# A block of attention and experts on one core: weight splitting, the last batch's scatters, shared inputs and results rearranged

## The chip, the core and the metric

The kernel runs on one core of a Trainium2 chip, as one launch. The metric is the device time of one execution, in microseconds. The engines are TensorE (PE), VectorE (DVE), ScalarE (ACT), GpSimd (POOL) and SyncE (SP); each runs its own list of instructions in order, and semaphores tie the lists together.

## The reference

The input x has 16 batches of 512 tokens with 128 features. The block is two sublayers, each with a residual and a layer norm behind it:

```python
q = plucker(q1, q2); k = plucker(k1, k2)        # 16 heads, 6 line coordinates each, unit length
attn = softmax(causal(q @ (J k)^T * 6**-0.5))
x1 = layernorm(x + (attn @ v) @ Wo.T + bo)
cw = top-2 of sigmoid(x1 @ Wr.T + rb), of 8 experts
out = expert_shared(x1) + sum_e cw[e] * expert_e(x1)   # expert: silu(x Wg^T) * (x Wu^T) @ Wd^T
y = layernorm(x1 + out)
```

There are nine experts with three matrices of 128 x 256 each: the shared one (number 0 in the weight buffer) and eight routed ones. Only the two chosen of the eight are computed for a token.

## The kernel before

**Attention stage.** One body per batch b, on every engine, from `over_batches` (L217): batches 0 to 3 are written out, 4 to 13 are a loop of two, 14 and 15 are written out. Heads go in four groups g, the scores of a group in five chunks of 128 x 1024 in PSUM. TensorE makes a chunk (`scores`, L662), ScalarE takes its exponential (`exps`, L1010), GpSimd puts zeros above the diagonal (`mask`, L540), TensorE weighs the values (`weigh`, L680), ScalarE copies the sum out. In the same body the next batch is prepared (projection, lines, norms, features: `line_terms` to `write_features` on VectorE; `transpose_feat` on TensorE and `copy_feat` on VectorE, one for each g) and the earlier ones are finished: batch b-1 is normalised and projected (`residual`, L1274), batch b-2 gets its layer norm (`norm_out`, which waits for GpSimd's power in `inv_std`, L536), is split into two fp16 halves (`split`, L1298) and goes to the router; batch b-3 gets its choice of experts (`choose`, `slots`), and GpSimd scatters its rows to the experts' regions in DRAM (`dispatch`, L240: 4 tiles of 128 tokens, 2 choices each, one indirect DMA for each). The row buffer `xrow` has two halves; `split` of batch c waits until the scatters of batch c-2 have landed.

**Weights.** ScalarE rounds an expert's weights, times 64, to fp16 (`raise_weights`, L1050); VectorE then subtracts to get the lower half (`lower_weights`, L1423). The raw weights of expert e lie where the halves of expert e+1 go, so the nine run strictly one after another.

**Shared stage.** A unit is 256 tokens. The shared expert has 32 units; 20 (EARLY) run after attention, while batches 14 and 15 are still being finished and scattered. A unit goes TensorE `gate_up`, ScalarE `gate`, VectorE `hidden`, ScalarE `high_half`, VectorE `low_half`, TensorE `down`, VectorE `add_shared` (counts `acc_done`). SyncE loads a unit's x1 and its transposed halves (`load_shared`, L402) into a ring of 8 slots, as soon as the unit 8 before has been added; `store_pads` (L416, eight DMAs) stands in SyncE's list between them.

**Rounds.** Six rounds of 14 units: 12 routed, and after each six a shared one. SyncE loads the rows of a routed unit when its ring slot is free (`routed`, L429, with a register load for the address); GpSimd scatters the result to `z_scratch`.

**Results.** For each batch, SyncE loads two choices' z (ring of 4); GpSimd adds them; VectorE adds that to `acc`, takes statistics, adds epsilon (`vareps2`, a tensor_scalar, L1586); GpSimd raises to the power -0.5 (L605); VectorE makes the shift (L1590); ScalarE makes the result (L1156) in one of two buffers and issues the store (L1160).

## Time and profile before

| | us |
|---|---|
| median of 3 runs (1009.05 to 1015.84) | 1010.12 |
| the profiled execution, its own time | 1010.27 |
| its span, first to last instruction | 1008.5 |
| PE busy | 767.6 (76%) |
| DVE busy | 704.4 (70%) |
| POOL busy | 628.5 (62%) |
| ACT busy | 588.6 (58%) |

The chain of work that ended last is 42% PE, 34% DVE, 11% issue, 5% ACT, 3% POOL and 2% DMA of the span. The stages follow one another in time: start and weights' first loads to 46 us, attention to about 650, the rest of the shared stage to 716, the rounds to 946, the results to the end. "Busy" leaves out waits and the issuing of DMAs; "idle before" is what an engine stood before an instruction, with what ended it.

### The profile page before, as it was taken

The numbers are of one execution on the slowest core, as the hardware profiler recorded it, in microseconds if no ns is written. First come the engines' busy times: TensorE is split into PE (matmuls) and PEld (weight loads), VectorE is DVE, ScalarE is ACT, GpSimd is POOL, SyncE is SP. The second block draws the span as 40 slices with busy tenths as digits, with TensorE's granted clock in tenths as the row PEclk, the third lists the DMA queues.
The fourth block names the chain that finished last, engine by engine and source line by source line (L and its number), as shares of the span: only waits on it lengthen the run. The fifth ranks groups of instructions, "written<-read, shape, count | busy, mean of one in ns | idle before, by whom it ended". The sixth has DMA issues, their size and how long they took to land.

```text
span 1008.5 us, 24870 instructions
## 1 busy us (share of the span) xinstructions
PE 767.6 (76%) x7672; PEld 481.7 (48%) x7673; DVE 704.4 (70%) x1858; ACT 588.6 (58%) x907; POOL 628.5 (62%) x914
## 2 busy tenths in 40 slices
PE   3468878879879879889879878667989989899100
PEld 2324444444444445344434434365878778788000
DVE  1665688797797787788788785476756656666394
ACT  0177677576576677567567668333456656666145
POOL 4155456686686686677676676525076666666594
PEclk9579899899899889889889889698999999999655
DMA  5000000110110110111011011325333333332483
GB/s 182 12 1 11 12 22 27 39 43 27 38 42 26 37 42 26 37 39 42 24 42 35 18 43 54 106 82 153 98 101 95 104 102 88 98 98 68 128 254 123
DMA packets 95055, 66.03 MB, mean 65 GB/s; under 512 B 9052, under 2 KB 87654, under 8 KB 94992
## 3 DMA queue, kind: packets, MB, share of 16 engines
q1 hardware_dynamic: 69328, 39.77, 14.0%
q0 software_dynamic: 8768, 17.07, 5.1%
q10 hardware_dynamic: 16896, 8.39, 2.8%
q8 instruction: 35, 0.57, 0.2%
q14 instruction: 28, 0.23, 0.1%
HBM read 34.50 MB, written 31.74 MB: 66 GB/s over the span
## 4 chain that ended last, share of the span: by engine, by line
PE 42%; DVE 34%; issue 11%; ACT 5%; POOL 3%; DMA 2%; SPq 2%; ACTq 1%; DVEq 1%; POOLq 0%
PE S L870 12%; PE O L690 8%; PE O L886 6%; PE W L655 5%; PE S L675 3%; DVE prodA L1218 3%; DVE rs_a L1242 2%; PE W L631 2%; DVE rs_b L1241 2%; DVE x L1294 1%; ACT p L1001 1%; DVE prodA L1223 1%; ACT probs L1016 1%; PE W L901 1%; DVE rden L1269 1%
## 5 line engine op out<-in xcount | busy, mean ns | idle before, releaser
L1016 ACT ACTIVATE probs<-S 128x1024 f32<-128x1024 f32 x320 | 322.8, 1033 | 171.0 <-PE S L675 124.2
L546 POOL TENSOR_SCALAR_AFFINE_SELECT probs<-probs 128x256 f32<-128x256 f32 (+1 forms) x448 | 220.6, 517 | 183.9 <-ACT probs L1016 183.1
L589 POOL DMA_INDIRECT z_scratch<-y,rows x144 | 146.4, 1016 | 100.5 <-ACT y L1104 63.2
L690 PE MATMUL O<-probs,v_aug 128*32 128x512 f32 (+3 forms) x2048 | 184.7, 482 | 4.7 <-POOL probs L546 4.7
L247 POOL DMA_INDIRECT rows_scratch<-xrow,slot_i x128 | 132.0, 1032 | 57.6 <-issue 32.1
L675 PE MATMUL S<-qkT 32*128 32x512 f16 (+3 forms) x1024 | 144.1, 323 | 14.9 <-ACT probs L1016 9.0
L1532 DVE TENSOR_TENSOR hid<-hid 128x512 f16<-128x512 f32 x104 | 72.0, 692 | 95.0 <-ACT hid L1131 94.2
L1112 ACT ACTIVATE silu<-S 128x512 f32<-128x512 f32 x104 | 62.1, 597 | 116.9 <-PE S L870 115.0
L870 PE MATMUL S<-xT_rt,w_T 128*128 128x256 f16 x864 | 107.9, 275 | 16.3 <-DVE xT_rt L1489 8.2
L886 PE MATMUL O<-w_T,hid 128*128 (+1 forms) x1248 | 96.8, 222 | 11.9 <-DVE hid L1532 10.5
L655 PE MATMUL W<-ident,feat 128*128 128x128 f16 x512 | 55.5, 276 | 57.1 <-DVE rt_logit L1311 40.5
L870 PEld LDWEIGHTS S<-xT_rt,w_T 128*128 x864 | 79.0, 98 | 30.9 <-issue 19.3
L675 PEld LDWEIGHTS S<-qkT 32*128 32x128 f16 x1024 | 39.0, 93 | 112.9 <-issue 45.6
L886 PEld LDWEIGHTS O<-w_T,hid 128*128 128x128 f16 x1248 | 79.1, 99 | 28.5 <-DVE acc L1496 10.1
L690 PEld LDWEIGHTS O<-probs,v_aug 128*32 128x32 f32 x2048 | 55.5, 114 | 77.1 <-issue 57.2
L655 PEld LDWEIGHTS W<-ident,feat 128*128 128x128 f16 x512 | 41.6, 124 | 94.2 <-DVE rt_logit L1311 44.3
L1261 DVE COPY qkT<-W 128x1024 f16<-128x1024 f16 x64 | 42.8, 687 | 61.6 <-PE W L655 61.5
L1509 DVE SCALAR_TENSOR_TENSOR hid<-silu,S 128x512 f32<-128x512 f32 x104 | 70.7, 679 | 0.0
L1131 ACT CAST hid<-hid 128x512 f16<-128x512 f32 x104 | 63.5, 610 | 8.7 <-DVE hid L1509 8.7
L534 POOL TENSOR_TENSOR prodB<-p 128x192 f32<-128x192 f32 (+2 forms) x96 | 55.8, 616 | 12.9 <-ACT p L1001 12.6
L1218 DVE TENSOR_TENSOR prodA<-p 128x192 f32<-128x192 f32 (+2 forms) x96 | 47.2, 579 | 21.8 <-ACT p L1001 21.8
L1023 ACT COPY oT_raw<-O 128x512 f32<-128x512 f32 x64 | 37.6, 588 | 33.6 <-PE O L690 33.5
(155 smaller groups left out, 1203.7 us busy)
## 6 DMA issues: line engine op xcount, KB each, us to landing
rows<-rows_scratch SPq DMA_DIRECT2D x72, 130.0 KB, 2.2
z<-z_scratch SPq DMA_DIRECT2D x32, 256.0 KB, 4.0
x_in<-in_L_attn_x ACTq DMA_DIRECT2D x16, 256.0 KB, 2.8
x_scratch<-x SPq DMA_DIRECT2D x16, 256.0 KB, 2.3
x1T_scratch<-x1T SPq DMA_DIRECT2D x16, 256.0 KB, 2.3
xT_sh<-x1T_scratch SPq DMA_DIRECT2D x32, 128.0 KB, 3.1
x_in<-x_scratch SPq DMA_DIRECT2D x32, 128.0 KB, 3.3
out<-res ACTq DMA_DIRECT2D x16, 256.0 KB, 2.9
```

The source lines that it names most:

```text
L247: pool.indirect_dma_start(out=rows_dram, in_=xrow[:, par, t, k, :], in_offset=None, out_offset=bass.IndirectOffsetOnAxis(ap=slot_i[:, par, ...
L546: pool.affine_select(out=v, in_=v, compare_op=ALU.is_ge, fill=0.0, base=0, pattern=[[0, v.shape[1]], [1, P]], channel_multiplier=-1).then_ ...
L589: pool.indirect_dma_start(out=z_dram, in_=y[:, q, a, :], in_offset=None, out_offset=bass.IndirectOffsetOnAxis(ap=rows[:, q, a, P + 1:P + 2 ...
L655: mm = pe.transpose(w[:, s, t * P:(t + 1) * P], feat[:, first:first + 4, :].rearrange("p h f -> p (h f)"), ident16[:, :])
L675: mm = pe.matmul(S[(g + c) % 2][:, col:col + T - kb * P], k, q, start=True, stop=True)
L690: mm = pe.matmul(O[g % 2][32 * j:32 * j + 32, kb * P:T], v_aug[:, par, kb, 4 * g + j, :], probs[:, g % 2, c, col:col + T - kb * P], start= ...
L870: mm = pe.matmul(S[r % 2][:, k * UNIT:(k + 1) * UNIT], weights(e, w, k), xT[:, a, :], start=(n == 0), stop=(n == 2))
L886: mm = pe.matmul(O[par][:, a * P:(a + 1) * P], hid16[:, par, h, k * UNIT + a * P:k * UNIT + (a + 1) * P], weights(e, w, 4 + k), start=(n = ...
L1016: act.activation(probs[:, g % 2, c, :], S[(g + c) % 2][:, :], ACT.Exp, scale=-SCALE / SPLIT_UP ** 2).then_inc(s_exp, 1)
L1218: ins = dve.tensor_tensor(dst, many, one, ALU.mult)
L1509: dve.scalar_tensor_tensor(out=hid[:, par, :], in0=silu[:, par, :], scalar=H_UP / UP ** 2, in1=S[par][:, 2 * UNIT:4 * UNIT], op0=ALU.mult, ...
L1532: dve.tensor_tensor(hid16[:, par, 1, :], hid[:, par, :], hid16[:, par, 0, :], ALU.subtract)\
```

## The change

1. **Weights.** `weights_at(b, k)` gives the nine pairs other places: (0,1), (0,2), (0,3), then (b,1) and (b,2) for b = 1, 2, 3. On VectorE each stands behind `copy_feat` of that number; on ScalarE behind the copy of group 1 (k=1), the exponentials 2 and 3 of group 3 (k=2), the last exponential (k=3).
2. **Split.** `split_done` is signalled after the lower half, before the copy for the second choice.
3. **Last batch.** GpSimd has an order of its own, `last_batch`; TensorE's transposes of batch 14 and ScalarE's copy of them go behind the batch's body; two of GpSimd's waits among the following scatters are gone.
4. **Shared inputs.** One load per batch (two units), four slots of twice the size; in the rounds both shared units use one slot, loaded once in a round.
5. **Results** are handled in pairs of batches: one epsilon addition, one power and one shift for two, four result buffers; the epsilon addition is a tensor_tensor with a tile `eps8`.

```diff
@@ GpSimd, last batch
+            def last_batch(b):
+                inv_std(b - 2)
+                mask(b, 0)
+                mask(b, 1, (0, 1))
+                dispatch(pool, b - 3, 0, (0,))
+                mask(b, 1, (2,))
+                dispatch(pool, b - 3, 0, (1,))
+                mask(b, 1, (3, 4))
+                dispatch(pool, b - 3, 0, (2,))
+                mask(b, 2, (0, 1, 2))
+                dispatch(pool, b - 3, 0, (3,))
+                mask(b, 2, (3, 4))
+                inv_std(b - 1)
+                mask(b, 3, (0, 1, 2, 3))
+                dispatch(pool, b - 2, 1, (0,), (0,))
+                mask(b, 3, (4,))
...
             dispatch(pool, NB - 3, 1, (1, 2))
-            pool.wait_ge(y_full, NB)
             dispatch(pool, NB - 3, 1, (3,))
             inv_std(NB - 1)
-            dispatch(pool, NB - 2, 0, (0,), (0,))
-            pool.wait_ge(logit_read, NB)
-            dispatch(pool, NB - 2, 0, (0,), (1,))
-            dispatch(pool, NB - 2, 0, (1, 2, 3))
+            dispatch(pool, NB - 2, 0, range(NT))
@@ TensorE, behind the last body
             pe.wait_ge(w_lo, NX)
+            transpose_x1(NB - 2, 0, NB - 3, NB - 2, True)
+            gate_up_early(0)
             router(NB - 2, 0)
             ranks(NB - 3, NB - 1)
-            gate_up_early(0)
@@ SyncE
+            def load_early(b):
...
+                if 2 * b >= SLOTS:
+                    sp.wait_ge(acc_done, 2 * b + 2 - SLOTS)
+                load_shared(b, b % (SLOTS // 2))
...
             def shared(i, p):
-                sp.wait_ge(acc_done, EARLY - EARLY % SLOTS + j + 1 if first else m - MIDS + 1)
-                load_shared(EARLY // 2 + MIDS // 2 * i + j // 2, j % 2, j)
+                if slot_at(p) == 0:
+                    first = isinstance(i, int) and i == 0
+                    sp.wait_ge(acc_done, 2 * (EARLY // 2 - SLOTS // 2) + 2 if first else number_at(i, p))
+                    load_shared(EARLY // 2 + i, MID_SLOT)
...
-            for m in range(SLOTS + 3, SLOTS + 5):
-                load_early(m)
+            load_early(5)
+            load_early(6)
             store_pads()
@@ VectorE, end of the body
                     for g in range(HP):
                         copy_feat(b + 1, 1 - par, g)
+                        lower_weights(b, g)
@@ VectorE, results
+            def pair(p, r, i):
+                add_routed(2 * p, 2 * r)
+                statistics(2 * p, 0)
+                add_routed(2 * p + 1, 2 * r + 1)
+                aggregate(2 * p, r, 0)
+                statistics(2 * p + 1, 1)
+                if not (isinstance(p, int) and p == 0):
+                    shift_pair(p - 1, 1 - r)
+                aggregate(2 * p + 1, r, 1)
+                dve.wait_ge(aggr_done, 2 * p + 2)
+                dve.tensor_tensor(vareps2[:, r, :], meanvar2[:, r, :, 1], eps8[:, :], ALU.add).then_inc(var2_done, 1)
@@ GpSimd, results
+            def pair(p, r, i):
+                for h in range(2):
+                    sum_choices(2 * p + h, 2 * r + h, i)
+                if not (isinstance(p, int) and p == 0):
+                    inv_std_pair(p - 1, 1 - r)
```

## Rows read from the trace of the kernel before

**Rows 1.** Stages: window, length, busy us (instructions) by engine, PE clock, DMA share, GB/s

```profile
608.00:650.30 42.30, 30.49 (x288) 13.47 (x284) 21.90 (x89) 27.11 (x32) 23.61 (x40) 0.76 0.31 90
715.70:945.70 230.00, 203.09 (x2331) 172.78 (x2328) 139.57 (x259) 131.83 (x314) 146.37 (x144) 0.98 0.32 90
945.70:1008.50 62.80, 0.00 (x0) 0.00 (x0) 40.80 (x176) 26.34 (x64) 40.32 (x32) 0.50 0.70 201
```

**Rows 2.** Timeline of DVE, batches 0 and 1: start, duration, instruction, idle before

```profile
81.30 0.69 DVE L1261 COPY qkT<-W 128x1024 f16<-128x1024 f16 x1 [1.89 <-PE W L655]
...
99.95 0.96 DVE L1428 SCALAR_TENSOR_TENSOR w_T<-w_T 128x768 f16<-128x768 f32 x1 [2.04 <-ACT w_T L1056]
...
118.24 0.69 DVE L1261 COPY qkT<-W 128x1024 f16<-128x1024 f16 x1 [2.48 <-PE W L655]
```

**Rows 3.** Timeline of PE, batches 1 and 2

```profile
109.53 0.62 PE L655 MATMUL W<-ident,feat 128*128 128x128 f16 x8 [3.21 <-DVE feat L1257]
...
112.13 1.94 PE L690 MATMUL O<-probs,v_aug 128*32 128x512 f32 x8
...
140.54 0.87 PE L757 MATMUL W<-ident,xrow 128*128 128x128 f16 x8 [4.09 <-DVE xrow L1306]
...
150.75 1.06 PE L690 MATMUL O<-probs,v_aug 128*32 128x512 f32 x8
```

**Rows 4.** Timeline of ACT, last exponential of batch 0

```profile
81.89 1.02 ACT L1016 ACTIVATE probs<-S 128x1024 f32<-128x1024 f32 x1 [0.52 <-PE S L675]
```

**Rows 5.** Timeline of POOL, last scatter of batch 12, power of batch 15

```profile
635.38 0.97 POOL L247 DMA_INDIRECT rows_scratch<-xrow,slot_i  x1 [0.30 <-issue]
...
665.48 1.08 POOL L538 TENSOR_TENSOR rstd<-vareps,minus_half 128x4 f32<-128x4 f32 x1
```

**Rows 6.** Timeline of DVE, split of batch 14, norm of batch 15

```profile
639.30 0.43 DVE L1303 TENSOR_SCALAR xrow<-x 128x512 f16<-128x512 f32 x1 [4.18 <-DMA rows_scratch<-xrow,slot_i]
...
666.59 1.29 DVE L1294 TENSOR_SCALAR x<-ysum,meanvar,rstd 128x128 f32<-128x128 f32 x4 [1.40 <-POOL rstd L538]
```

**Rows 7.** Timeline of PE, last weighing, gate block of shared unit 13

```profile
650.27 2.36 PE L690 MATMUL O<-probs,v_aug 128*32 128x512 f32 x32 [1.09 <-POOL probs L546]
...
699.56 1.84 PE L870 MATMUL S<-xT_sh,w_T 128*128 128x256 f16 x12 [3.13 <-DMA x_in<-x_scratch]
```

**Rows 8.** Timeline of DVE, round 1: the second shared unit of round 0 added

```profile
760.58 0.41 DVE L1496 SCALAR_TENSOR_TENSOR acc<-O,x_in 128x256 f32 x1
```

**Rows 9.** Timeline of SP, round 1: the first shared load

```profile
748.32 0.60 SPq L403 DMA_DIRECT2D xT_sh<-x1T_scratch  x1
```

**Rows 10.** Timeline of PE, rounds: transposes of round 1, a gate block of round 3

```profile
765.57 0.39 PE L901 MATMUL W<-ident,rows 128*128 128x128 f16 x4
...
827.06 2.74 PE L870 MATMUL S<-xT_rt,w_T 128*128 128x256 f16 x12 [1.69 <-DVE xT_rt L1489]
```

**Rows 11.** Line 434, the 71 row loads between 706 and 910 us

```profile
DMA to landing us min/median/max: 2.1/2.2/2.6
```

**Rows 12.** Groups by line, DVE, results: busy us, mean ns, idle before

```profile
L1586 DVE TENSOR_SCALAR vareps<-meanvar 128x4 f32<-128x4 f32 x16 | 12.8, 800 | 0.0
...
L1590 DVE SCALAR_TENSOR_TENSOR shift<-meanvar,rstd 128x4 f32<-128x4 f32 x16 | 2.4, 151 | 2.6 <-POOL rstd L605 2.6
```

**Rows 13.** Timeline of all engines, results, 957 to 959 us

```profile
957.55 1.25 POOL L599 TENSOR_TENSOR z<-z 128x512 f32<-128x512 f32 x1
957.62 1.21 DVE L1586 TENSOR_SCALAR vareps<-meanvar 128x4 f32<-128x4 f32 x1
```

**Rows 14.** Timeline of ACT, first and last batch of the results

```profile
961.75 0.49 ACT L1156 ACTIVATE res<-acc,shift,rstd 128x128 f32<-128x128 f32 x1 [24.17 <-DVE shift L1590]
...
1003.93 1.65 ACT L1156 ACTIVATE res<-acc,shift,rstd 128x128 f32 x4 [0.74 <-DMA out<-res]
```

**Rows 15.** Line 1160, the result stores: who waited for them (us, times)

```profile
  ACT res L1156: 13.0, 10
```

**Rows 16.** Stages, four microseconds of the results; columns as in rows 1

```profile
976.00:980.00 4.00, 0.00 (x0) 0.00 (x0) 3.94 (x20) 1.81 (x5) 3.90 (x4) 0.50 1.02 293
```

More of the change, by code:

```diff
@@ L238, in ahead, with weights_at @@
             return not (isinstance(b, int) and b + 2 >= NB)
+        def weights_at(b, k):
+            places = ([(0, 3)] if NX % 2 else []) + [(c, g) for c in range(PEEL) for g in (1, 2)]
+            return sorted(places).index((b, k)) if isinstance(b, int) and (b, k) in places else None
+        assert NX == 2 * PEEL + 1
         def dispatch(pool, c, par, tiles, choices=(0, 1)):
@@ L355, in block_program, with over_pairs @@
         assert NSH == EARLY + MIDS * ROUNDS and NRT == NRING * ROUNDS and NRING == 2 * TURN and ROUND == 14
-        def over_results(eng, body, after):
-            for b in range(ZRING):
-                body(b, b, 0)
-            with eng.Fori(1, NB // ZRING) as i:
-                for r in range(ZRING):
-                    body(ZRING * i + r, r, i)
-            for b in range(NB, NB + after):
-                body(b, b % ZRING, b // ZRING)
-        RES_AHEAD = 2
-        def there(b):
-            return not isinstance(b, int) or 0 <= b < NB
-        assert NB % ZRING == 0
+        NPAIR = NB // 2
+        def over_pairs(eng, body):
+            body(0, 0, 0)
+            body(1, 1, 0)
+            with eng.Fori(1, NPAIR // 2) as i:
+                body(2 * i, 0, i)
+                body(2 * i + 1, 1, i)
+        assert NB % 4 == 0 and ZRING == 4
         block = ctx.enter_context(nc.Block())
@@ L1076, in body @@
                 copy_out(b, 0)
-                raise_weights(b, 1)
                 exps(b, 1, (4,))
@@ L1592, in _, with add_routed, statistics @@
-            over_results(dve, finish, 3)
+            def add_routed(b, slot):
+                dve.wait_ge(zsum_done, b + 1)
+                batch = acc[:, bass.ds(NT * b, NT), :]
+                dve.tensor_tensor(batch, batch, z[:, slot, 0], ALU.add).then_inc(tot_done, 1)
+            def statistics(b, h):
+                dve.wait_ge(tot_done, b + 1)
+                dve.sem_inc(parted, 1)
+                for t in range(NT):
+                    src = acc[:, bass.ds(NT * b + t, 1), :].rearrange("p o d -> p (o d)")
+                    ins = dve.bn_stats(stats2[:, NT * h + t, :], src)
+                ins.then_inc(stats2_done, 1)
```

217 lines of the change are left out of this document (96 added, 121 removed).

## The prediction, made before the changed kernel was run

> **What bounds the kernel now.** I read the stages first [rows 1], then in each stage the timeline of the engine that waits, to see which wait ends last. The mean hides four different limits. While attention runs (to 608 us), the next batch's features on VectorE and the scores on TensorE take turns. In the last attention batch (608 to 650) TensorE is busy 30.5 of 42.3 us at a mean clock of 0.76: a stage of waits. In the routed rounds (716 to 946) it is busy 203 of 230 us: TensorE-bound. In the results stage it does nothing, while VectorE and GpSimd are busy throughout and ScalarE 26 of 63 us.
>
> **Part A, splitting the weights.** Nine pairs of a ScalarE and a VectorE instruction (0.96 us [rows 2]) sat three to a batch in batches 0 to 2; now batch 0 has three and batches 1 to 3 two, between the copies of the transposed features. Before, VectorE stood 2.04 us for ScalarE's half in front of the norms [rows 2], again 2.04 in batch 2. In batch 1 the wait and the instruction held the features up 2.9 us, and TensorE waited 3.21 us for them [rows 3]. That goes: -2.9. Behind such a gap its 8-matmul block took 1.94 us where it takes 1.06 at the full 2.4 GHz (112.13 and 150.75 [rows 3]); a shorter gap may spare it, between 0 and 2.5 us, I take 1.2, for the 1 us of gap that I leave. In batch 2 the same 3.0, plus 0.7 of the first instruction (the rest of it would be a wait for GpSimd's products), fall inside TensorE's wait of 4.09 us [rows 3]: -3.7. Batch 0: -1.4, from one ScalarE instruction off its path (0.75) and a short feature wait (0.7).
>
> What it costs: the new places have idle time, but not everywhere. Copy 2 has over 2 us after it; its weights wait for a ScalarE instruction that stands behind the exponentials of chunk 3, so copy 3 (118.24 [rows 2]) slips by 0.3 to 0.9. Copy 3 releases the transposes, the copy of x, the residual and the next load, hence the next batch's first exponential: +0.8 in each of batches 1 to 3, less 0.9 at the start of batch 3 where the old instruction stood in front of the expert choice. In batch 0 the third pair waits for the last exponential (81.89 + 1.02 [rows 4]), so ScalarE ends at 83.8, VectorE at 84.8, and the copy of x, which followed copy 3 (81.30 [rows 2]) at 82.73, starts at 84.8: +2.1. Sum: batch 0 +0.7, batch 1 -3.3, batches 2 and 3 -2.9 (-3.7 + 0.8 + 0.8 - 0.9, rounded): **-5.5**, bounds -9 and 0. Signalling the split before its second copy saves 0.43 us only where TensorE waits for it; it is inside the figures.
>
> **Part B, last batch and hand-over.** VectorE can't overwrite the row buffer until batch 12's scatters have landed. GpSimd issues the last at 635.38; VectorE stands 4.18 us for it and starts at 639.30 [rows 5, 6]. The new order starts the scatters after two masks of group 1 instead of three. A tile is two of 0.97 + 0.30 us [rows 5], the masks between are as before, so the last is issued near 630.3 and lands near 634.2; VectorE's normalisation then ends last, at 634.5: 4.8 us sooner. TensorE's transposes and ScalarE's copy move behind the scores, so the last scores no longer wait for them, but the router now comes after the first gate block: 0.8 back. The final mask stays behind batch 13's first scatter, hence weighing, 650.27 before [rows 7], moves by **-4.0** (bounds -2.8, with the gate block at half clock, and -5.9). Next, seven scatters of batch 13 follow without the wait for the projection (9 us, cover until 655), so the power of batch 15 (1.08 us [rows 5]) no longer waits behind one, and VectorE's 1.40 us wait for it [rows 6] goes: **-1.4**. Batch 14's eight scatters now run beside VectorE's normalising: +0.3, estimated. SyncE: before, unit 13's input was queued behind eight pad stores, and TensorE waited 3.13 us for it [rows 7]. Now units 12 and 13 go ahead together, the pads start 3 us later (they stand behind a wait for six additions), and units 14 and 15 land near 701.1, where unit 14 started at 702.5: **-1.6**, bounds 0 and -2.5. Fewer DMA issues on SyncE are worth nothing: it is idle there. Part B: **-6.7**, bounds -3.5 and -9.5.
>
> **Part C, shared inputs in the rounds.** Two half loads on two slots become one load on one slot, which must wait until both shared units of the round before are added. In round 1 that addition starts at 760.58 and takes 0.41 [rows 8]; SyncE came to this place at 748.3 [rows 9], so now it stands 13 us, and behind it are the row loads. The first of them must have landed when TensorE transposes at 765.57 [rows 10]: 5.0 us after the addition began. (From the trace's other rounds the distance is the same within 0.1; five rounds have it.) The path is 0.4 addition, 0.3 wake, 0.9 to 1.3 two issues, 0.8 register load, 2.2 to 2.6 landing [rows 11]: 4.6 to 5.4, or up to 7.3 if the rows queue behind the 512 KB ahead. So the stall is 0 to 2.3 us in each of five rounds; I take 0.4, as the landings of that queue hardly spread: **+2**, bounds 0 and +12.
>
> **Part D, results.** Before, VectorE spends 0.80 us in the mean on an addition of four numbers [rows 12]. The reason is beside it: the one of 957.62 ends at 958.83, GpSimd's addition at 958.80 [rows 13]. It is held until GpSimd is done. Now it is one per two batches and a tensor_tensor. The one other small instruction with two inputs, shift, took 0.151 us in the mean of 16 [rows 12] beside the same GpSimd work, so I price the new one so. VectorE then needs about 2.0 us a batch. GpSimd's four instructions for two batches become three; the power of eight numbers costs between 1.08 and twice that, so at most 2.4 a batch. ScalarE becomes the bound: 1.65 + 0.74 [rows 14] = 2.4. Its pace was (1003.93 - 961.75) / 15 = 2.81, since it waited 13.0 us in ten places for a result buffer to be stored [rows 15]; four buffers end that. 15 x 0.41 = 6.1; the first pair is ready near 960.4, 1.3 sooner, though one shift now serves two. **-7.3**, bounds -3.4 and -8.6.
>
> **Sum** -5.5 - 6.7 + 2 - 7.3 = -17.5. The profiled execution took 1010.27 us (span 1008.5 and 1.8 around it), 0.15 above the median of 1010.12. **Forecast 993 us**, chance 0.58, its own range 986 to 1000.
>
> **Rivals.**
> 1. The DMA engines bound the results. At 976 us they are fully busy at 293 GB/s [rows 16]; a batch moves 786 KB, so 2.4 us would need 328 GB/s. For: the row. Against: input loads run ahead and end early, and the stores catch up later. At 2.67 us a batch part D is 15 x 0.14 + 1.3 = -3.4: 997 us. Chance 0.13.
> 2. The two-input addition is held as well. Then one hold of some 0.9 us per pair keeps VectorE at 2.5 us a batch, ahead of ScalarE's 2.4, and the adds stretch GpSimd's: part D about -5, 995 to 996 us. Against it stand the 16 shifts; chance 0.09. The Trainium skill, GPSIMD Engine Reference, Specifications, speaks for it: GpSimd shares its SBUF interfaces with VectorE, and instructions with two SBUF inputs contend as those in a 2-port mode do. By that rule the swap of forms buys nothing.
> 3. Part A gives nothing, because the batch ends lose what the norms gain: 998 to 999 us. For: copy 3 is on the path. Chance 0.12.
> 4. Slower: SyncE's new wait. If the row loads land 4 us or more after issue behind 512 KB, TensorE idles some 2.5 us in each of five rounds, and its clock falls: at 827.06, after 1.69 us idle, a gate block took 2.74 us instead of 1.48 [rows 10]. Stall, clock and the refilled pipeline then make 4.5 a round: 991 + 22 = 1013 us. It turns the sign from 3.9 us a round. Against: slack before the wait was so measured that only queueing brings it. Chance 0.04; milder, at 1000 to 1005 us, 0.04.
>
> **Range and chances.** 8 in 10 over these: 985 to 1002 us. A change of under about 1% is what this kernel's measurement can't tell from none. Faster by over 1% means below 1000.0: the forecast nearly whole, most of rivals 1 and 2, half of 3: 0.78. Within 1%: 0.19. Slower: 0.03.
>
> **What would show it.** A: no VectorE wait for ScalarE's weights, TensorE's feature wait in batch 1 near 1 us; batch 0 as long as before. B: VectorE's wait for scatters gone, the weighing of group 3 near 641 (645 or 646 less A's 5.5), a TensorE wait of some 3 us at unit 14. C: SyncE standing 13 us a round, TensorE's row transposes waiting under 1 us. D: the small addition near 0.15 us, ScalarE's results every 2.4 us without a wait for stores. I am wrong if scatters beside VectorE stretch its work, if the round waits exceed 1 us, or if results come slower than every 2.6 us.

## The result, and the profile after

The changed kernel takes 1002.45 us (median of 15 runs, 996.83 to 1005.49), the kernel before 1007.98 us (15 runs, 998.57 to 1017.2): ratio 0.9946, 95% interval 0.9926 to 0.9965. It is faster by half a per cent. 993 us was forecast, with a range to 1002: the time lies just outside, and of the 17.5 us forecast about 5.5 came. The profiled execution took 1001.03 us (span 999.3); the one of before 1010.27, which is 2.3 above its later median. So the two traces differ by 9.2 us, and one trace of each kernel is not enough for a stage: the figures of this section are held against ten more traces below.

How far each stage moved (each stretch from the first instruction named to the next; five rounds: from round 0's first silu to round 5's):

| us | before | after | forecast | measured |
|---|---|---|---|---|
| start to first exponential | 46.68 | 45.54 | 0 | -1.1 |
| batches 0 to 3 (part A) | 151.17 | 146.06 | -5.5 | -5.1 |
| batches 4 to 14 | 411.12 | 411.91 | 0 | +0.8 |
| batch 15's first exponential to round 0's first silu (part B) | 110.57 | 109.44 | -6.7 | -1.1 |
| five rounds (part C) | 182.43 | 185.09 | +2 | +2.7 |
| round 5's first silu to the first z load | 43.76 | 44.09 | 0 | +0.3 |
| first z load to the end (part D) | 62.78 | 57.14 | -7.3 | -5.6 |

The rows of after that answer to [rows 1], from the stages view (window, length, busy us and instructions of PE, PEld, DVE, ACT and POOL, PE clock, DMA share, GB/s):

```profile
603.50:642.00 38.50, 29.10 (x284) 12.70 (x288) 22.50 (x90) 26.31 (x32) 24.11 (x41) 0.84 0.32 98
709.00:930.00 221.00, 201.37 (x2286) 170.60 (x2285) 137.00 (x254) 128.45 (x306) 138.43 (x136) 0.99 0.32 89
942.00:999.30 57.30, 0.00 (x0) 0.00 (x0) 35.64 (x160) 26.34 (x64) 35.63 (x24) 0.50 0.77 220
```

The limits are the same as before. What is new lies between the first two windows. **Part A** took the wait in batch 1 away, as forecast: the timeline of PE in batch 1, answering to [rows 3]:

```profile
106.86 0.62 PE L672 MATMUL W<-ident,feat 128*128 128x128 f16 x8 [0.37 <-DVE feat L1277]
...
109.29 1.06 PE L707 MATMUL O<-probs,v_aug 128*32 128x512 f32 x8
```

The wait for features is 0.37 us where it was 3.21, and the 8-matmul block runs in 1.06 us instead of 1.94. Batch 1 is 4.5 us shorter in this pair of traces (3.3 forecast), batch 2 1.4 shorter.

**The hand-over.** GpSimd and PE around the last weighing, answering to [rows 5, 7]:

```profile
639.45 1.03 POOL L254 DMA_INDIRECT rows_scratch<-xrow,slot_i  x1 [5.98 <-DVE slot_i L1372]
640.50 0.65 POOL L546 TENSOR_SCALAR_AFFINE_SELECT probs<-probs 128x512 f32<-128x512 f32 x1
```

```profile
641.21 4.49 PE L707 MATMUL O<-probs,v_aug 128*32 128x512 f32 x32 [3.74 <-POOL probs L546]
645.64 2.15 PE L885 MATMUL S<-xT_sh,w_T 128*128 128x256 f16 x12
...
694.27 2.74 PE L885 MATMUL S<-xT_sh,w_T 128*128 128x256 f16 x12 [5.17 <-DMA x_in<-x_scratch]
```

The weighing starts at 641.21, as forecast. But TensorE now stands 3.74 us before it, for a mask that stands on GpSimd behind a scatter, which waits 5.98 us for its slots. And behind the gap the weighing takes 4.49 us instead of 2.36, the gate block 2.15 instead of 1.47. The stages view has the granted clock of this stretch:

```profile
641.21:648.00 6.79, 6.79 (x48) 3.30 (x49) 1.74 (x8) 0.77 (x2) 5.15 (x6) 0.57 0.12 41
```

0.57 of full speed is little above the lower level of 1.2 GHz, and the weighing alone (641.21 to 645.64) had 0.50. Then, at shared unit 14, comes a wait of 5.17 us for an input, and again a block at the lower level (2.74 us). SyncE's timeline shows why:

```profile
678.27 0.43 SPq L407 DMA_DIRECT2D x_in<-x_scratch  x1
679.74 8.65 SPq L421 DMA_DIRECT2D rows_scratch<-pad_rows  x8
688.51 0.40 SPq L405 DMA_DIRECT2D xT_sh<-x1T_scratch  x1
688.96 0.45 SPq L407 DMA_DIRECT2D x_in<-x_scratch  x1
```

The load of units 12 and 13 goes at 677.89, after the sixth addition; the eight pads fill SyncE until 688.4; only then is units 14 and 15's load issued, and it lands at 694.2, 5.3 us after the issue of its second half.

**Rounds.** SyncE stands from 742.4 to 755.67 for the addition, 13 us as forecast. The row transposes never waited for rows before. Now they do; the line's own view has matmuls and weight loads together:

```profile
  DMA rows<-rows_scratch: 3.0, 9
```

Four of the nine waits are of matmuls, 1.1 us in all; the other five are of weight loads, which run beside matmuls.

**Results.** Groups by line for VectorE, answering to [rows 12]:

```profile
L1616 DVE TENSOR_TENSOR vareps<-meanvar,eps 128x8 f32<-128x8 f32 x8 | 5.0, 624 | 0.3
L1603 DVE SCALAR_TENSOR_TENSOR shift<-meanvar,rstd 128x8 f32<-128x8 f32 x8 | 2.7, 340 | 1.7 <-POOL rstd L615 1.7
```

The addition for a pair was to take 0.15 us and takes 0.62, and the shift has grown from 0.15 to 0.34. The timeline of all engines shows the same picture as [rows 13], in the new form, and now for the shift as well:

```profile
952.45 1.26 POOL L608 TENSOR_TENSOR z<-z 128x512 f32<-128x512 f32 x1 [0.46 <-DMA z<-z_scratch]
952.47 1.27 DVE L1616 TENSOR_TENSOR vareps<-meanvar,eps 128x8 f32<-128x8 f32 x1
...
960.43 2.48 POOL L608 TENSOR_TENSOR z<-z 128x512 f32<-128x512 f32 x2
961.87 1.07 DVE L1603 SCALAR_TENSOR_TENSOR shift<-meanvar,rstd 128x8 f32<-128x8 f32 x1
```

952.47 + 1.27 = 953.74, 0.03 us after GpSimd's addition ends; 961.87 + 1.07 = 962.94, again 0.03 us after (960.43 + 2.48). Both are held. The results come every 2.49 us (2.40 forecast, 2.81 before), and none waits for a store any more. The DMA engines did not bound them either:

```profile
970.00:980.00 10.00, 0.00 (x0) 0.00 (x0) 9.53 (x45) 6.62 (x17) 9.19 (x7) 0.50 1.11 322
```

322 GB/s over ten microseconds, where [rows 16] had shown 293 at a share of 1.02. Rival 1 of the prediction, which took 293 for the ceiling, is refuted.

### The profile page after: what moved, and what is told of

Read it like the earlier page. It is cut to its first block, busy times and chain, and to the rows that moved or that the text cites. A ratio compares the mean times of both kernels' runs of the same rounds, so it can differ in the third digit from the quotient of the medians.

```text
span 999.3 us, 24749 instructions
## 1 busy us (share of the span) xinstructions
PE 766.2 (77%) x7672; PEld 480.2 (48%) x7673; DVE 700.7 (70%) x1842; ACT 588.0 (59%) x907; POOL 623.6 (62%) x907
## 4 chain that ended last, share of the span: by engine, by line
PE 39%; DVE 32%; issue 12%; ACT 6%; DMA 3%; POOL 2%; SPq 2%; ACTq 1%; DVEq 1%; POOLq 0%
PE S L885 10%; PE O L707 8%; PE W L672 5%; PE O L901 5%; PE S L692 4%; PE W L648 3%; DVE prodA L1238 3%; DVE rs_a L1262 2%; ACT res L1177 2%; DVE rs_b L1261 2%; DVE x L1314 1%; DVE feat L1271 1%; ACT hid L1149 1%; DVE rden L1289 1%; DVE rs_b L1260 1%
## 5 line engine op out<-in xcount | busy, mean ns | idle before, releaser
L600 POOL DMA_INDIRECT z_scratch<-y,rows x144 | 146.9, 1020 | 110.6 <-ACT y L1122 74.0
L672 PE MATMUL W<-ident,feat 128*128 128x128 f16 x512 | 55.1, 274 | 67.2 <-DVE rt_logit L1332 54.2
L672 PEld LDWEIGHTS W<-ident,feat 128*128 128x128 f16 x512 | 41.3, 124 | 105.1 <-DVE rt_logit L1332 58.1
L1042 ACT COPY oT_raw<-O 128x512 f32<-128x512 f32 x64 | 37.5, 586 | 33.0 <-PE O L707 32.0
```

Source lines behind the costliest of these rows:

```text
L600: pool.indirect_dma_start(out=z_dram, in_=y[:, q, a, :], in_offset=None, out_offset=bass.IndirectOffsetOnAxis(ap=rows[:, q, a, P + 1:P + 2 ...
L672: mm = pe.transpose(w[:, s, t * P:(t + 1) * P], feat[:, first:first + 4, :].rearrange("p h f -> p (h f)"), ident16[:, :])
```

## The experiments

Seventeen runs of thirteen kernels, each timed beside the kernel before on the same chip. The theory: the loss is SyncE's. With one load per batch, the load of units 12 and 13 stands for one addition more, the pads behind it, units 14 and 15 behind the pads. Rivals: the order on GpSimd; the size of the loads; that the gains of A or D are not there.

The chips were not alike. On two, and where the result was measured, the kernel before took 1007.5 to 1010 us ("usual"), on two others 1084 and 1094 ("slow"): there the rounds are longer, and the traces don't show by what. Seven of the runs fell on the slow ones, and four of those kernels were run again. The stretches of the runs on usual chips, from the profile of each (one execution):

| kernel | batches 0 to 3 | batches 4 to 14 | batch 15 to round 0 | of it from the first silu | five rounds | first z load to last result | ratio |
|---|---|---|---|---|---|---|---|
| before | 151.2 | 411.1 | 110.6 | 70.3 | 182.4 | 59.9 | 1 |
| after | 146.1 | 411.9 | 109.4 | 74.3 | 185.1 | 54.0 | 0.9946 |
| a_alone | 143.0 | 413.9 | 110.8 | 70.9 | 182.8 | 57.5 | 0.9953 |
| c_again | 147.9 | 407.5 | 115.4 | 76.3 | 185.8 | 58.1 | 1.0064 |
| d_alone | 148.3 | 411.0 | 111.1 | 71.5 | 183.9 | 53.9 | 0.9924 |
| no_c | 146.7 | 415.3 | 103.6 | 68.9 | 182.8 | 54.6 | 0.9841 |
| pads_first | 142.8 | 410.8 | 106.7 | 71.6 | 183.8 | 54.2 | 0.9897 |
| mask_first | 146.7 | 414.3 | 101.1 | 67.7 | 184.5 | 54.6 | 0.9836 |
| form | 146.6 | 412.2 | 109.5 | 74.4 | 184.2 | 53.4 | 0.9923 |
| best1_again | 146.1 | 411.9 | 100.1 | 65.0 | 182.4 | 53.6 | 0.9829 |
| ring5_again | 142.9 | 414.2 | 102.2 | 67.1 | 184.3 | 53.3 | 0.9861 |
| best3_again | 146.7 | 412.4 | 97.6 | 62.7 | 185.4 | 54.8 | 0.9820 |

The table also shows how far a stretch moves by itself. Where the code is the same, batches 0 to 3 took 147.9 to 151.2 us (before, c_again, d_alone) and batches 4 to 14 took 407.5 to 411.1 in the same three; the hand-over took 110.6 to 111.1 (before, a_alone, d_alone), and the results 57.5 to 59.9 (before, a_alone, c_again).

**a_alone**: before, with part A's edits only.

> The kernel before with part A alone (the weights' places, and the split signalled before its second copy). Theory 1, by the stages of the two profiles: batch 0 longer by 1.1 us, batch 1 shorter by 4.5, batch 2 by 1.4, batch 3 by 0.3, nothing behind: 5 us less in all, ratio 0.995. Theory 2 (rival 3 of the prediction: the ends of the batches lose what the norms gain, and the 5 us in the changed kernel's profile are chance or come of another part): the first four batches take the 151.2 us of before within 1 us, ratio 1.000.

Measured: 0.9953 [0.9930, 0.9976], a gain of 2.4 to 7.1 us. Theory 1 holds by the ratio, and rival 3's "nothing" lies outside the interval. The four batches took 143.0 us here and 146.1 in the changed kernel, because batch 0 took 35.3 against 39.2 (taken up in the last section) and batch 2 one more. In the traces the gain is less plain. Batch 1, 36.9 us in the trace of before, took 35.0 in c_again and d_alone, whose code there is that of before, and 32.2 to 32.5 in the nine kernels with part A. Over batches 0 to 3 the means are 149.1 us without part A (three traces) and 145.3 with it (nine): -3.9. But over batches 4 to 14 they are 409.9 and 413.0: +3.1. Of part A only the earlier signal of the split is in these batches; whether it costs this, or the traces spread so, no run here settles.

**no_c**: the changed kernel without part C.

```diff
-            def load_shared(b, slot):            # whole batch, 4 slots
+            def load_shared(b, half, slot):      # 256 tokens, 8 slots
...
-            load_early(5)
-            load_early(6)
-            store_pads()
-            for b in range(7, EARLY // 2):
-                load_early(b)
+            for m in range(SLOTS + 3, SLOTS + 5):
+                load_early(m)
+            store_pads()
+            for m in range(SLOTS + 5, EARLY):
+                load_early(m)
```

> The changed kernel without its part C: half loads into eight slots, and SyncE's order of the kernel before (unit 12, the pads, unit 13), and two loads a round into two slots. Theory 1 (part C costs time in both places): the six round starts come 35.8 to 37.6 us apart, 2 to 3 us less over five rounds than in the changed kernel (185.1), SyncE does not stand for an addition in a round, and the row transposes never wait; TensorE waits again some 3 us at unit 13 instead of 5.17 at unit 14; time 4 to 6 us below the changed kernel, ratio to the kernel before about 0.989. Theory 2 (the rounds are longer for another reason, and the wait behind the pads is of the same size with half loads, because TensorE comes to it earlier): rounds as in the changed kernel, wait 5 us or more, ratio 0.994 to 0.996.

Measured: 0.9841 [0.9809, 0.9873], more than theory 1 had. Timeline of PE, unit 13:

```profile
692.54 1.48 PE L886 MATMUL S<-xT_sh,w_T 128*128 128x256 f16 x12 [1.91 <-DMA x_in<-x_scratch]
```

A wait of 1.91 us at unit 13, at full clock, in place of 5.17 at unit 14. Against the changed kernel the stretch to round 0 is 5.8 us shorter and the rounds 2.3. In these two stretches part C costs the changed kernel 8.1 us by this pair of traces; the medians are 7.3 us apart (1002.45 and 995.11, not taken beside each other), the ratios 10.6. Of the 5.8 us, 3.5 are that the pads end later against batch 15's start (84.9 us behind it, 81.4 in no_c), and 2.1 that the whole-batch load lands 5.8 us behind the last pad (688.40, 694.22) where no_c's half load lands 3.7 behind (688.83, 692.50). So the later wait is the larger part, and the size of the load has a share. So what is left of B in this stretch is 103.6 against 110.6: -6.9 us.

**c_again** (and c_alone): before, with part C only.

> The kernel before with part C alone. Theory 1 (a direct cost of the loads: 2.3 us over five rounds, and in the shared stage the load of units 12 and 13 waits for a sixth addition, 3 us later, and with it the pads and units 14 and 15): rounds longer by 2 to 3 us, the stretch from the first silu to round 0 longer by 1 to 4 us, ratio 1.003 to 1.007. Theory 2 (part C costs nothing by itself; it hurt the changed kernel only because TensorE reached unit 14 earlier there): rounds longer by 2 to 3 us and the stretch within 1 us of the 70.3 us before, ratio 1.002 to 1.003.

c_alone ran on the slow chip: 0.9944 [0.9903, 0.9984], against both theories. It was run again.

> The kernel c_alone once more, since it ran on a chip on which the kernel before takes 1084 us and the rounds are stretched by a third, whatever the kernel; there its ratio was 0.994. Theory 1 (part C costs by itself): where the kernel before takes about 1010 us, rounds longer by 2 to 3 us, the stretch from the first silu to round 0 longer by 1 to 4 us, ratio 1.003 to 1.007. Theory 2 (it hurts only where TensorE comes early to unit 14, as behind part B): the stretch within 1 us of before, ratio 1.000 to 1.003. If the chip is the slow one again: 0.990 to 0.998, and no word on either.

Measured: 1.0064 [1.0033, 1.0095], slower, as theory 1 had it. From the first silu to round 0 it takes 76.3 us, 6.0 more than in before and above the 1 to 4 that I expected; from batch 15's start it is 4.8 more than in before and 4.3 more than in d_alone:

```profile
698.21 2.74 PE L869 MATMUL S<-xT_sh,w_T 128*128 128x256 f16 x12 [5.55 <-DMA x_in<-x_scratch]
```

The wait at unit 14 is there without part B, so it is not TensorE's haste that makes it. On a chip of the other kind, where the stretch is long for other reasons, part C is no loss; why it was a gain there stays open.

**b_alone**: before, with part B's orders only.

> The kernel before with part B's orders alone (GpSimd's, TensorE's and ScalarE's in the last batch and behind it); SyncE's loads are those of before. Theory 1, from the changed kernel without part C, where the stretch from batch 15's first exponential to round 0's first silu took 103.64 us against 110.57: 6 to 7 us less, all in this stretch, ratio 0.993 to 0.994. Theory 2 (part B gained there only together with the weights or the results): the stretch within 2 us of 110.6, ratio 0.998 to 1.000.

It ran on the slow chip: 0.9954 [0.9911, 0.9996]. That is a gain, of a size between the two theories; there is no trace of before on that chip to set its stretch against. The size rests on no_c.

**pads_first**: the changed kernel with the pads one place earlier.

```diff
             load_early(5)
-            load_early(6)
             store_pads()
+            load_early(6)
```

> The changed kernel with the eight pad stores moved ahead of the load of units 12 and 13. In the changed kernel SyncE stored the pads from 679.74 to 688.4 and issued the load of units 14 and 15 behind them (688.51, x1 landed 694.22), and TensorE waited 5.17 us for it and then ran its block in 2.74 us where 1.47 is usual. Theory 1 (that queue is what ate part B): pads from about 672.6 to 681.3, units 12 and 13 land near 685, units 14 and 15 near 688, the wait is under 1 us, and the stretch from the first silu to round 0 goes from 74.3 to 68 to 69 us; time 5 to 6 us less, ratio to the kernel before about 0.989. Theory 2 (a load of 256 KB for two units is simply slow, or the stretch's end is set by VectorE's table or the scatters of batch 15): the wait only moves to unit 12 or to the first rows, the stretch stays at 73 to 75 us, ratio 0.994 to 0.995.

Measured: 0.9897 [0.9863, 0.9931]; the stretch from the first silu 71.6 us, between the theories.

```profile
683.88 2.74 PE L885 MATMUL S<-xT_sh,w_T 128*128 128x256 f16 x12 [3.42 <-DMA x_in<-x_scratch]
```

The wait is gone from unit 14 and 3.42 us of it stand at unit 12, whose load is now behind the pads (issued 678.1). The ratio fits theory 1, but its interval is 7 us wide; the stretch decides, and it gave 2.7 us where 5 to 6 were expected. This left open whether SyncE's wait or the size of the loads is to blame.

**ring5_again** (and ring5): the changed kernel with `SLOTS = 10`, five pair slots, and nothing else; the load of units 12 and 13 waits for four additions instead of six.

> The changed kernel with five pair slots in place of four, nothing else: the load of units 12 and 13 then waits for four additions and not for six, so SyncE comes to the pads when their addresses are there (about 672.5) and is through them at 681.3; the load of units 14 and 15 is issued 7 us earlier. Theory 1 (the step that failed is this: the load of units 12 and 13 is held for a sixth addition, the pads behind it, units 14 and 15 behind the pads): no TensorE wait for a shared input over 0.5 us before the rounds, the stretch from the first silu to round 0 from 74.3 to 67.5 to 69 us, rounds unchanged at 184 to 186 us over five; time 5 to 6 us under the changed kernel's, ratio 0.988 to 0.990. Theory 2 (a load of two units lands late by its size, or something else holds the stretch's end): a wait of over 2 us stays, the stretch 71 us or more, ratio 0.992 to 0.995.

ring5 ran on a slow chip: 0.9774 [0.9702, 0.9847], with no TensorE wait for a shared input left. Run again:

> The kernel ring5 once more: its first runs, on a slow chip (the kernel before 1094 us), had no TensorE wait for a shared input left, but the stretches of that chip can't be set beside the changed kernel's. If the chip is the usual one (the kernel before about 1008 us). Theory 1 (SyncE's wait for the sixth addition is the cause): the stretch from the first silu to round 0 67.5 to 69 us against 74.3, ratio 0.988 to 0.990. Theory 2 (the size of the loads): 71 us or more, ratio 0.992 to 0.995.

Measured: 0.9861 [0.9815, 0.9907]; the stretch from the first silu is 67.1 us against 74.3. SyncE and PE of ring5_again:

```profile
668.00 0.47 SPq L407 DMA_DIRECT2D x_in<-x_scratch  x1
672.99 8.97 SPq L421 DMA_DIRECT2D rows_scratch<-pad_rows  x8
682.53 0.45 SPq L407 DMA_DIRECT2D x_in<-x_scratch  x1
```

```profile
686.45 1.47 PE L885 MATMUL S<-xT_sh,w_T 128*128 128x256 f16 x12
688.43 1.47 PE L885 MATMUL S<-xT_sh,w_T 128*128 128x256 f16 x12
```

The load of units 12 and 13 goes at 668 instead of 678, the pads start as soon as their addresses are there, units 14 and 15 are loaded at 682.5, and unit 14 (the second PE row) follows unit 13 without a wait. The loads are as large as in the changed kernel, and units 14 and 15 still land 5.2 us after their issue (682.53, 687.71), but now in time. Theory 1 is shown: without the wait in front of the pads the loss is gone. The 7.3 us are more than the 5.8 that part C costs here (no_c), since waiting for four additions also ends unit 13's old wait for an input, 1.91 us in no_c.

**mask_first**: pads_first, and on GpSimd

```diff
-                mask(b, 3, (0, 1, 2, 3))
+                mask(b, 3)
                 dispatch(pool, b - 2, 1, (0,), (0,))
-                mask(b, 3, (4,))
```

> The kernel pads_first, and on GpSimd the last mask of batch 15 ahead of batch 13's first scatter. In the changed kernel the exponential that the mask needs ended at 635.4, the scatter waited for its slots until 639.45, and the mask behind it released the weighing at 641.21, after 3.74 us of TensorE waiting; the weighing then took 4.49 us where it took 2.36 before, the gate block 2.15 instead of 1.47. Theory 1 (order and the half clock behind the gap cost all of this): weighing at about 637.5, taking 2.4 to 3 us, gate block of unit 1 4 to 6 us earlier, time 4 to 6 us below pads_first. Theory 2 (VectorE's choice of experts for batch 13, until 639.2, or its scatters set the following steps, so that TensorE only waits later): the weighing is early but the first unit's down projection and the silu of unit 5 come at the same time as in pads_first within 1.5 us, time 0 to 1.5 us less.

Measured: 0.9836 [0.9803, 0.9870]. The median is 2.9 us below that of pads_first (994.6, 997.5), the ratio 6 us; the stretch decides, 101.1 us against 106.7. Timeline of PE:

```profile
639.12 2.36 PE L706 MATMUL O<-probs,v_aug 128*32 128x512 f32 x32
641.41 1.48 PE L884 MATMUL S<-xT_sh,w_T 128*128 128x256 f16 x12
```

No wait, 2.36 us, and the gate block at full clock. Theory 1: the stretch is 5.6 us shorter. The gap and the clock behind it (2.1 and 0.7 us) are all given back, although TensorE now waits 3.79 us for an input at unit 12, where it waited 3.42.

**d_alone** and **form**: before with part D only; the changed kernel with the epsilon addition as a tensor_scalar.

> The kernel before with part D alone. By the results stage of the changed kernel: first result 15.0 us after the first z load instead of 16.0, one result every 2.5 us instead of 2.8, 5 to 6 us less, ratio 0.994 to 0.995. Rival (the pairs gained there because the part before them was different): 1 to 3 us, ratio 0.997 to 0.999.

> The changed kernel, but the epsilon addition for a pair is a tensor_scalar again (one input from SBUF and a constant) in place of the tensor_tensor with eps8. Theory 1 (either form is held while GpSimd adds z: in the kernel before the tensor_scalar of 128x4 ended 0.03 us after GpSimd's addition each time, in the changed one the tensor_tensor of 128x8 did): mean 0.6 to 0.65 us, six of eight held, the results stage 57 us, time as the changed kernel's within 1 us, ratio 0.994 to 0.995. Theory 2 (the tensor_scalar alone is held, as I took it in the prediction, and the tensor_tensor for another reason): mean and stage differ from the changed kernel's by over 0.3 us and 1 us.

d_alone: 0.9924 [0.9893, 0.9955]. form: 0.9923 [0.9899, 0.9948]. In form five of the eight additions are held (0.68 to 0.81 us), each until GpSimd's addition ends, and three take 0.17, two of them with no such addition under way and one that began at the same time as it:

```profile
L1616 DVE TENSOR_SCALAR vareps<-meanvar 128x8 f32<-128x8 f32 x8 | 4.2, 529 | 0.3
```

The means differ by 0.1 us and the two intervals of the ratio overlap; either form is held, in five of eight places here where six were expected. The results stage of before's trace (59.9) is the longest of the kernels without D (57.5 and 58.1 in a_alone and c_again; mean of the three 58.5); the nine with D have 53.3 to 54.8 (mean 54.0). So part D is worth 4.4 us by the means, and 5.8 by the one pair.

**best1_again** (and best1): no_c, the mask as in mask_first, the pads ahead of the load of unit 12. **best2**: best1, with the epsilon addition on GpSimd.

> The changed kernel without part C, with GpSimd's last mask ahead of batch 13's first scatter, and with the pads ahead of the load of unit 12 (each half load then has no pads in front of it by the time that its unit comes up). Theory 1 (the two effects add: 5.6 us between pads_first and mask_first in the stretch from batch 15 to round 0, and 1.91 us of waiting at unit 13 in no_c): the stretch takes 96 to 97 us where no_c took 103.6, no wait for a shared input over 0.5 us, time about 988 us, ratio 0.977. Theory 2 (with TensorE that early, another thing is late: VectorE's choice of experts and table for batch 15, or the landing of its scatters and of the first rows): the stretch takes 99 to 101 us, ratio 0.980 to 0.982.

> The kernel best1 once more, beside the kernel before, since its first runs (ratio 0.975) were on the slow chip. If the chip is the usual one: the stretch from batch 15's first exponential to round 0's first silu 96 to 98 us (no_c 103.6), ratio 0.976 to 0.979, time about 988 us. If part of its gain there was the chip's: the stretch 99 to 101 us, ratio 0.980 to 0.983.

> The kernel best1, and in the results GpSimd itself adds epsilon, with one tensor_scalar of 128x8 in front of its power; VectorE has no such addition any more. In the changed kernel VectorE's addition took 0.624 us in the mean where 0.17 is its length with GpSimd idle, and the first of them 1.27 us. Theory 1 (an instruction of VectorE with two SBUF inputs is held while GpSimd adds z): the first result comes 1 to 1.4 us earlier after the first z load, the rest stays at ScalarE's pace of 2.4 to 2.5 us a batch, 1.5 to 2.5 us less than best1, ratio 0.002 lower. Theory 2 (GpSimd is the next limit: two additions of 1.26, a power of 1.9 and the new instruction): results every 2.6 us or slower, no gain or up to 2 us of loss against best1.

best1 on the slow chip: 0.9750 [0.9696, 0.9804]; best1_again: 0.9829 [0.9801, 0.9858], the stretch 100.1 us, of which 2.35 is a wait at unit 12 behind the pads. So neither the 96 to 97 of theory 1 nor another engine: it is the pads once more. best2, beside best1: 0.9726 [0.9672, 0.9780], not told apart from it in time. Its results stage shows that theory 1 failed in its mechanism, in the timeline of all engines:

```profile
1006.60 2.47 POOL L607 TENSOR_TENSOR z<-z 128x512 f32<-128x512 f32 x2
1006.65 1.23 DVE L1602 SCALAR_TENSOR_TENSOR shift<-meanvar,rstd 128x8 f32<-128x8 f32 x1 [0.52 <-POOL rstd L617]
...
1008.09 1.53 DVE L1583 TENSOR_TENSOR acc<-acc,z 128x512 f32 x1
1009.05 0.67 POOL L613 TENSOR_SCALAR vareps<-meanvar 128x8 f32<-128x8 f32 x1
```

The first result did not come earlier but 1.0 us later than in best1 (16.4 us after the first z load, 15.4). With the one held instruction gone from VectorE, the next ones are held: the shift took 1.23 us, and the addition to `acc`, 0.68 us elsewhere, took 1.53: it ended 0.55 us after GpSimd's two additions were over (1009.07). It holds in the other direction too: GpSimd's own small addition took 0.67 us beside it, and 0.26 with no such work under way. The hold isn't bound to an instruction and moves on when that is taken away.

**best3_again** (and best3): best1 with the pads in two lots.

```diff
             load_early(SLOTS + 3)
-            store_pads()
-            for m in range(SLOTS + 4, EARLY):
+            store_pads(range(5))
+            for m in range(SLOTS + 4, SLOTS + 7):
+                load_early(m)
+            store_pads(range(5, NE))
+            for m in range(SLOTS + 7, EARLY):
                 load_early(m)
```

> The kernel best1 with the pads in two lots: five ahead of the load of unit 12, three behind the load of unit 14. In best1 TensorE waited 2.35 us at unit 12, whose input was issued at 678.23 behind eight pads. Theory 1: unit 12 is issued 3.3 us earlier and no wait for a shared input is over 0.5 us, the stretch from batch 15 to round 0 97.5 to 98.5 us (100.1 in best1_again), ratio 0.980 to 0.981. Theory 2 (the second lot only moves the wait to units 15 or 16): the stretch 99.5 us or more, ratio 0.982 to 0.984.

> The kernel best3 once more, for the same reason. On the usual chip: no wait for a shared input over 0.5 us, the stretch from batch 15's first exponential to round 0's first silu 97.5 to 98.5 us against 100.1 in best1_again, ratio 0.980 to 0.982, the fastest of all. If the second lot of pads moves the wait: 99.5 us or more, ratio 0.982 to 0.984.

best3 on a slow chip: 0.9768 [0.9706, 0.9829]. best3_again: 0.9820 [0.9773, 0.9866], 989.25 us; the stretch 97.6 us, no wait for a shared input, as theory 1 has it. In time it can't be told from best1_again (989.11 us): its trace has five rounds of 185.4 us where best1_again has 182.4, with the same code there. **ring5_mask**, ring5 with the early mask, ran on the slow chip alone:

> ring5 with GpSimd's last mask ahead of batch 13's first scatter. Theory 1: the stretch from batch 15's first exponential to round 0's first silu takes 97 to 99 us (changed kernel 109.4, best1_again 100.1 with a wait of 2.35 us left), ratio 0.981 to 0.984, the 3 us of the rounds being all that part C still costs. Theory 2 (with no wait for inputs, VectorE's choice of experts or the rows of round 0 take over): the stretch 100 us or more, ratio 0.984 to 0.987.

0.9807 [0.9743, 0.9871], with no wait for a shared input; the stretches can't be compared. best1 and best3 beat both kernels: 1.7 to 1.8% below the kernel before on usual chips, where the changed one is 0.5% below it.

## Why the prediction was wrong, step by step

**Part A: the mechanism seen, the size not settled.** The waits of TensorE that I named in batches 1 and 2 (3.21 and 4.09 us) are gone, but in batch 3, where I had expected no VectorE wait for ScalarE's weights, there is one of 1.64 us (187.20), and batch 3 takes 39.1 to 39.9 us in the nine traces with part A where c_again and d_alone have 37.5. -5.5 was forecast; the pair of traces has -5.1, a_alone's ratio -4.7 (-7.1 to -2.4), and the means over twelve traces -3.9, with +3.1 behind it in batches 4 to 14, which I had put at nothing. That the pair came so near is in part luck: before's trace was the longest of its kind in batches 0 to 3.

**Part B: its orders gained, not where I said.** Without part C the stretch gains 6.9 us; the steps on GpSimd, TensorE and VectorE were forecast at -5.1 (-4.0, -1.4, +0.3). In the changed kernel the weighing moved by -3.6 against batch 15's start (37.7 us behind it, 41.3 before). But it and the gate block lost 2.8 us to the lower clock, so that at the block's end only -0.8 was left. That lies outside my bound of -2.8, which allowed for the gate block alone. I had seen that the mask stays behind the scatter, and priced the shift of the start but not the gap in front of it; mask_first gives 5.6 us back. From there to unit 12 the order gained 3.1 us more (-3.9 at unit 12), where -1.1 was forecast: batch 15's norm follows GpSimd's power without a wait.

**The step that failed** is the one on SyncE: "the pads start 3 us later (they stand behind a wait for six additions), and units 14 and 15 land near 701.1, where unit 14 started at 702.5: -1.6". In the changed kernel -3.9 at unit 12 became -1.1 at round 0: +2.8 for -1.6. The chain was the right one and each link too short. In c_again, put on the clock of before by batch 15's start (601.61 there, 608.97 before), the pads start at 690.7 and not at 689; from their end to the landing it takes 5.6 us where my 701.1 left 3.4; the input lands at 705.6. (1.6 of the pads' 4.8 us is that TensorE is that much later at unit 12 already, which d_alone shows too, with the old loads.) And I set it against unit 14's old start of 702.5, which was itself late by unit 13's wait of 3.13 us [rows 7], a wait that the edit removes. So TensorE stands 5.55 us. I even wrote that a wait of "some 3 us" would show, and put no clock to it; the block behind it took 2.74 us where it had been 2.20. ring5_again gives 7.3 us back by one more slot, of which 5.8 are part C's. I had looked for the price of the new waits in the rounds, where they are easy to see, and not at the ring's other wait, in front of the pads; the bounds 0 and -2.5 left a loss out without a reason.

**Part C in the rounds: right.** SyncE stands 13 us; the matmuls of the row transposes wait 0.3 to 1.3 us in all, over the rounds, in the six traces on the usual chips that have part C, and never in the six without. Five rounds take 183.8 to 185.8 us with it and 182.4 to 183.9 without, but 185.4 once (best3_again); the mean difference is about 1.3 us, where +2 was forecast.

**Part D: the mechanism right, a term mis-sized.** -5.6 us for -7.3 in the pair, -4.3 by the means over twelve traces. The pace is 2.49 us and not 2.40 (15 x 0.09 = 1.4 us). The first result comes 1.0 us sooner in the pair, where I had 1.3, but that is not shown to be part D's: it comes 15.2 to 16.0 us after the first z load in the three traces without D and 14.4 to 15.8 in the nine with it. The error of reading is instructive: I priced the new addition at 0.15 us "beside the same GpSimd work", since the 16 shifts took 0.151. Looked at one by one, twelve of the 16 start 0.06 us before the end of GpSimd's addition, because each follows a held addition of epsilon, and the other four start beside none. They never met the lock; their mean said nothing of it. Rival 2 was the case, and its -5 lies between the -5.6 of the pair and the -4.3 of the means. By the rule that I cited for it, the Trainium skill, GPSIMD Engine Reference, Specifications (shared interfaces, contention of two-input instructions), this was to be expected, and the traces agree: 1.27 us for an addition of eight numbers per lane. The Trainium skill, Trainium Architecture — The Big Picture, What this means for kernel authors, calls it an exclusive lock and no split of bandwidth; best2 agrees, where instructions were drawn out to 1.23 and 1.53 us on VectorE and to 0.67 on GpSimd until the other engine was done; GpSimd's power is an exception (last section).

The sum of the miss, by the traces: 5.6 us in part B's stretch (3.2 at the weighing, 4.4 at SyncE's step, less the 2.0 that came unforecast between them), 1.7 in D, 0.7 in C, 0.4 in A: 8.4, which is 17.5 - 9.2 within rounding. Between the medians another 3.7 us are missing: the profiled execution of before was 2.3 us above its median, the one of after 1.4 below. That the largest loss, part B's, is the loads' and the gap's is shown by ring5_again and mask_first; this split to the microsecond rests on one pair of traces. With the means over traces that have the same code it reads: A -3.9 and +3.1 behind it, B's stretch -1.3 (110.8 before, 109.5 in the changed kernel and form), C +1.3, D -4.3, in all -5.1, where the medians gave -5.5. By these the miss is 5.4 us in B's stretch, 4.7 in A and what follows it, and 3.0 in D, less 0.7 in C.

## What to carry to other kernels

Where loads are merged, look for each wait of the merged load, and for all that stands behind it on its queue: here one addition more in front of 9 us of pads, and a load twice as large behind them, cost 5.8 us, and one more slot gave 7.3 back. A start time read off the old trace is no due time if the same edit removes a wait ahead of it. A mean of short instructions "beside" another engine's work is evidence only if each of them started inside that work: check their starts against its ends.

## What the runs showed of the hardware

**The lock between VectorE and GpSimd.** While GpSimd adds two SBUF tiles (1.26 us for 128x512), small instructions of VectorE on SBUF wait for its end: a tensor_scalar (0.57 to 1.21 us for 0.17), a tensor_tensor (to 1.27), a scalar_tensor_tensor (to 1.23), and a 128x512 addition (1.53 for 0.68). Statistics of one input (0.87 us for four) were not stretched. It is not the kind of instruction alone that decides, but also which began first: in form an addition of epsilon that began together with GpSimd's took 0.17, and in the changed kernel GpSimd's addition, begun at 981.99, 0.03 us behind VectorE's 128x512 addition (0.69), took 1.78 instead of 1.26.

GpSimd's power is a case of its own. The timeline of the results of before has it both ways:

```profile
964.75 0.69 DVE L1569 TENSOR_TENSOR acc<-acc,z 128x512 f32 x1
964.78 1.54 POOL L605 TENSOR_TENSOR rstd<-vareps,minus_half 128x4 f32<-128x4 f32 x1 [0.18 <-DVE vareps L1586]
...
967.66 1.02 POOL L605 TENSOR_TENSOR rstd<-vareps,minus_half 128x4 f32<-128x4 f32 x1
967.71 0.70 DVE L1569 TENSOR_TENSOR acc<-acc,z 128x512 f32 x1
```

Begun 0.02 to 0.08 us behind VectorE's addition, the power took 1.49 to 1.54 us (eight times in this trace); begun 0.05 us ahead of it, 1.02 (six times), and VectorE's addition its usual 0.69 or 0.70 either way. So the power is held by the addition and doesn't hold it, though it too has two SBUF inputs.

**TensorE's clock at the start.** Batch 0, with the same code in all kernels that have part A, took 39.2 to 39.7 us in six profiles on usual chips and 35.3 to 35.4 in three. Stages view of the first 4.5 us, the changed kernel and pads_first:

```profile
45.50:50.00 4.50, 4.50 (x16) 3.36 (x15) 0.00 (x0) 2.59 (x3) 0.81 (x2) 0.53 0.22 64
```

```profile
45.50:50.00 4.50, 3.27 (x26) 2.17 (x24) 1.42 (x3) 4.46 (x6) 2.18 (x5) 1.00 0.23 64
```

The same work starts at 0.53 or at 1.00 of full clock, and 3.9 us of a single profile hang on it. Batches 4 to 14 spread more: 410.8 to 415.3 us in the nine kernels with part A, with the same code there. So a stage is read from several traces before less than 4 or 5 us are believed.

**Chips differ by 8%.** On two chips the kernel before took 1084 and 1094 us. The slowness is not everywhere: the same kernel best1 took 534.2 us for batches 0 to 14 there and 558.1 on the usual chip. But its five rounds took 250.5 us (182.4 on the usual chip), with engines standing for nothing that the trace shows, as ScalarE's silu here:

```profile
802.30 0.60 ACT L1126 ACTIVATE silu<-S 128x512 f32<-128x512 f32 x1 [2.68 <-issue]
```

Part C was slower on one kind of chip (1.0064) and faster on the other (0.9944). What delays the instructions there stays open. A ratio taken on one such chip isn't carried to the other.
